# Deformable-convolution stage of a four-layer kernel: block transposes and the second image's offset products change places

## The reference

```python
x = x + L0(gn(x))   # 3-channel offset conv, bilinear sampling, depthwise + pointwise conv
x = x + L1(gn(x))   # 3x3 average pool, then the deformable convolution below
x = x + L2(gn(x))   # 3x3 convolution with masked sign weights
x = x + L3(gn(x))   # striped spatial attention with two 1-d strip kernels
```

```python
xp     = avg_pool3(gn(x))
offset = conv2d(xp, off_w, off_b)            # 18 channels: dy, dx of 9 taps
mask   = 2 * sigmoid(conv2d(xp, mod_w, mod_b))   # 9 channels
# for each tap k and pixel: xp sampled bilinearly at (y + ky - 1 + dy, x + kx - 1 + dx),
# times mask, and out = sum over taps and channels with w; plus bias
```

## Time and profile before

| | |
|---|---|
| median of 3 runs | 1859.02 us (1857.61 to 1861.42) |
| the profiled execution | 1859.19 us |
| its span, first to last instruction | 1857.4 us |
| mean granted TensorE clock | 0.970 |
| busy: TensorE | 1678.3 us (90%) |
| busy: VectorE | 1192.2 us (64%) |
| busy: ScalarE | 603.5 us (32%) |
| busy: GpSimd | 82.9 us (4%) |

### The profile page before, as it was taken

The page is one execution under the profiler, slowest core; times in us unless marked ns, Lnnn a source line. Parts: engine busy times, 40 slices in busy tenths (PEclk is TensorE's granted clock), DMA queues, the critical chain, the costliest instruction groups (busy, mean ns, idle before and its releaser), DMA issues.

```text
span 1857.4 us, 23906 instructions
## 1 busy us (share of the span) xinstructions
PE 1678.3 (90%) x7908; PEld 866.5 (47%) x7908; DVE 1192.2 (64%) x2227; ACT 603.5 (32%) x986; POOL 82.9 (4%) x92
## 2 busy tenths in 40 slices
PE   4968999899998999999998899989999999998876
PEld 2535543455435553364534545355543555435422
DVE  5276359844698358983498734985459835797356
ACT  2134123341324313252242512444133441324222
POOL 1010000100000000000001000010000000000000
PEclk8989999999999999999999999999999999999987
DMA  2000000100000000100001000010000100000000
GB/s 106 12 12 2 1 1 1 48 1 1 1 13 36 1 1 1 43 6 1 1 1 48 2 1 1 1 48 1 1 1 1 47 2 1 1 23 1 1 0 23
DMA packets 7121, 22.97 MB, mean 12 GB/s; under 512 B 1233, under 2 KB 1937, under 8 KB 6929
## 3 DMA queue, kind: packets, MB, share of 16 engines
q1 hardware_dynamic: 6928, 20.58, 3.0%
HBM read 12.19 MB, written 8.39 MB: 11 GB/s over the span
## 4 chain that ended last, share of the span: by engine, by line
issue 74%; PE 16%; DVE 4%; POOL 3%; ACT 2%; POOLq 0%; DVEq 0%; ACTq 0%
PE psN L460 3%; PE psO L460 2%; POOL gst L418 2%; PE psO L486 2%; PE psN L806 1%; PE psN L486 1%; PE psN L561 1%; PE ps L470 1%; PE psN L682 1%; PE psO L682 1%; POOL strip L426 1%; ACT xq L890 1%; PE psN L590 1%; DVE samp L1518 1%; ACT samp L890 1%
## 5 line engine op out<-in xcount | busy, mean ns | idle before, releaser
L486 PE MATMUL psO<-samp,w 128*128 128x512 f32 x576 | 273.5, 605 | 20.8 <-ACT samp L890 20.8
L486 PE MATMUL psN<-xn,w 128*128 128x512 f32 x576 | 277.4, 605 | 5.9 <-issue 4.5
L590 PE MATMUL psN<-GQt,xq 64*128 64x144 f32 x2048 | 169.8, 305 | 25.2 <-ACT samp L890 24.2
L890 ACT ACTIVATE samp<-psN 128x576 f32<-128x576 f32 x256 | 154.2, 649 | 89.2 <-PE psN L590 87.8
L590 PEld LDWEIGHTS psN<-GQt,xq 64*128 64x128 f32 x2048 | 141.1, 190 | 56.8 <-ACT samp L890 42.1
L486 PEld LDWEIGHTS psO<-samp,w 128*128 128x128 f32 x576 | 100.5, 190 | 116.0 <-issue 104.2
L1053 ACT ACTIVATE samp<-psN,vec 128x512 f32<-128x512 f32 x160 | 110.1, 688 | 130.1 <-PE psN L806 130.1
L1217 DVE COPY xblk<-psN 120x256 f32<-120x256 f32 x128 | 54.3, 424 | 149.1 <-PE psN L526 148.8
L486 PEld LDWEIGHTS psN<-xn,w 128*128 128x128 f32 x576 | 98.8, 189 | 87.3 <-issue 85.1
L682 PE MATMUL psN<-img,w 128*128 128x512 f32 x288 | 134.1, 611 | 4.5 <-PE psO L544 4.5
L682 PE MATMUL psO<-img,w 128*128 128x512 f32 x288 | 132.9, 603 | 0.0
(11 more groups left out here) (142 smaller groups left out, 2328.6 us busy)
## 6 DMA issues: line engine op xcount, KB each, us to landing
xin<-in_x SPq DMA_DIRECT2D x16, 512.0 KB, 4.0
out<-yout SPq DMA_DIRECT2D x16, 512.0 KB, 3.5
w<-in_w SPq DMA_DIRECT2D x2, 576.0 KB, 5.4
samp<-in_r SPq DMA_DIRECT2D x1, 576.0 KB, 7.1
tab<-in_tab SPq DMA_DIRECT2D x1, 494.0 KB, 4.9
kh_w<-in_kh SPq DMA_DIRECT2D x1, 320.0 KB, 5.4
kv_w<-in_kv SPq DMA_DIRECT2D x1, 320.0 KB, 5.7
woT<-in_woT SPq DMA_DIRECT2D x1, 256.0 KB, 6.5
```

Source lines behind the costliest of these rows:

```text
L486: last = mm(dst[:, h, :], wgt[:, k, :], rhs(h, k), start=(k == 0), stop=(k == K9 - 1))
L590: last = mm(pair(u)[:, g, :].rearrange("p (k r c) -> p k r c", k=K9, c=SW)[:, :, :, cols], xQ[rows, t, a, e, :], w[rows, e, :, :, cols], s ...
L890: return nc.scalar.activation(out, in_, ACT.Copy)
```

## The change

TensorE waits for both outputs of the previous pass directly behind `offset_parts(2)`, and does blocks 0 and 1 before `offsets(2)`, blocks 2 and 3 behind it, and blocks 4 to 7 behind `doubles(0)`. Only then come `offset_parts(3)` and `far(2)`. `offsets(3)` moves from ahead of the branch into `near(0)`, behind the second step of tile 3; ahead of the branch TensorE now waits for its input (`parts_ready`). ScalarE copies blocks 0 to 3 behind `parts(2)`, then makes the mask, then copies blocks 4 to 7, then does `parts(3)`; for image 1 its order is as before. VectorE does `store_ready(1)` directly behind `store_ready(0)`, ahead of the box sums of image 1. The signal `y_ready` begins at 1 in place of 2, since its value "one of the two" is no longer waited for.

```diff
--- before.py
+++ after.py
@@ -229,7 +229,7 @@
         weights_ready = sem("weights_ready")
         w2_landed = sem("w2_landed")
         x_landed = [Signal(sem(f"x_landed{s}"), 16, 0) for s in range(2)]
-        y_ready = signal("y_ready", 2, 2)
+        y_ready = signal("y_ready", 2)
         yout_free = signal("yout_free", 2)
         y_stored = [Signal(sem(f"y_stored{s}"), 16, 0) for s in range(2)]
 
@@ -700,23 +700,26 @@
                 pe.wait_ge(added.sem, added.at(i, 2))
                 pe.wait_ge(pooled_ready.sem, pooled_ready.at(i, 1))
                 offset_parts(2, img[0], w1off)
+
+                pe.wait_ge(y_ready.sem, y_ready.at(i, 0))
+                blocks(i, 0, (0, 1))
                 offsets(i, 2, 27)
+                blocks(i, 0, (2, 3))
                 doubles(i, 0)
-
-
-                pe.wait_ge(y_ready.sem, y_ready.at(i, -1))
+                blocks(i, 0, range(4, TILES))
+
                 pe.wait_ge(pooled_ready.sem, pooled_ready.at(i, 2))
                 offset_parts(3, img[1], w1off)
                 far(i, 2)
 
-                pe.wait_ge(y_ready.sem, y_ready.at(i, 0))
-                blocks(i, 0, range(TILES))
-                offsets(i, 3, 27)
+                pe.wait_ge(parts_ready.sem, parts_ready.at(i, 4))
                 for s in range(2):
 
                     wait_apart(pe, (added, added.at(i, 2)), (far_ready, far_ready.at(i, s + 2)))
                     is_far = pe.value_load(flag[s][0:1, 0:1])
                     with pe.If(is_far > 0):
+                        if s == 0:
+                            offsets(i, 3, 27)
 
                         pe.wait_ge(g_strips.sem, g_strips.at(i, s + 1))
                         image_T(s, g_xTp)
@@ -730,7 +733,7 @@
 
                         pe.sem_inc(q_smp.sem, STEPS)
                     with pe.Else():
-                        near(i, s)
+                        near(i, s, lambda t: offsets(i, 3, 27) if s == 0 and t == 3 else None)
 
                         pe.wait_ge(q_smp_sb.sem, q_smp_sb.at(i, STEPS * (s + 1)))
 
@@ -981,17 +984,17 @@
                 order = EVENTS if more else LAST
                 parts(i, 2)
                 for s in range(2):
-                    if s:
-                        blocks(i, s, range(2))
+                    early = 2 if s else 4
+                    blocks(i, s, range(early))
                     act.wait_ge(om2_ready.sem, om2_ready.at(i, s + 1))
                     for e in range(PAIRS):
                         ins = nc.scalar.activation(mk[s][:].rearrange("p (t e k) -> p t e k", e=PAIRS, k=K9)[:, :, e, :],
                                                    om2[:, e, 2, :].rearrange("p (t k) -> p t k", k=K9),
                                                    ACT.Sigmoid)
                     ins.then_inc(mask_ready.sem, 1)
+                    blocks(i, s, range(early, TILES))
                     if s == 0:
                         parts(i, 3)
-                    blocks(i, s, range(2 * s, TILES))
                     if s and more:
                         normalise(i, "S0", order)
                         wide(i + 1, 0, i, order)
@@ -1604,10 +1607,10 @@
                     affine_scale(own, "L1B", order)
                     pool3(own, 0, 3, i, order)
                 store_ready(0)
+                store_ready(1)
                 if more:
                     for part in range(4):
                         pool3(own, 1, part, i, order)
-                store_ready(1)
                 if more:
                     assert own.n == DVE_STEPS, own.n
```

## The result

The changed kernel takes 1879.98 us, the median of 4 runs (1877.19 to 1881.84), beside 1858.38 us for the kernel before on the same chip (4 runs, 1857.61 to 1861.42). The ratio is 1.0112, with a 95% interval of 1.0093 to 1.0131: slower by 21.6 us. The forecast was 1884 us in a range of 1864 to 1900. The profiled execution took 1877.19 us, with a span of 1875.3 us and a mean granted clock of 0.965.

What follows compares the result with a forecast made beforehand. TensorE's list was taken to bound the kernel, VectorE's chain having 2.45 us to spare. Eight passes of 1.35 us (10.8) and 1.74 us (13.9) gave +24.7 us on 1859.2 us: 1884 us, range 1864 to 1900.

Steps and rivals of the forecast that it cites:

- TensorE's list isn't the path any more: Ahead of near(0): blocks and parts leave TensorE's path; VectorE's chain, as long, becomes the path; TensorE idles 570.3 to 575.1.
- make `doubles` late: Blocks 2 and 3 behind offsets(2): doubles starts 0.4 us late, VectorE's chain 0.2 us late, with 0.4 as bound.
- The strip copy blocks the hats for 1.95 us: GpSimd's second strip copy, let go earlier, falls inside VectorE's hats and delays them by 1.95 us.
- `near(0)` starts 0.2 us earlier: Start of the sampling: VectorE has tile 0 ready at 575.05, so near(0) starts at 575.1 instead of 575.33.
- `offsets(3)` inside costs 1.55 us: In near(0): these products cost 1.80 us and save a wait of about 0.25, so +1.55 us.
- +1.35 a pass: Convolution over samples: starts at 589.8 instead of 588.48, put at 1.35 us later in each pass.
- The clock loss of 1.74 us a pass: In near(0): after 4.8 us of TensorE idling the clock falls once each pass, +1.74 us; bounds 0 and 3.5.
- A: Rival: no clock loss in the sampling, only the first term, 1870 us; chance 0.17.
- B: Rival: a second clock loss from offsets(3) in the middle of near(0), +13.9 us on top, 1898 us; chance 0.20.
- C: Rival: strip copy doesn't delay the hats; 1854 us without clock loss (chance 0.09), 1868 us with one (0.08).
- D: Rival: no effect, the losses and the gains of C cancel, 1859 us; chance 0.05.

Runs made afterwards that it cites:

- experiment 1: The changed kernel, with GpSimd's strip copy for image 1 waiting until all eight GQt tiles of image 0 are made: 1866.43 us, ratio 1.0034.
- experiment 11: The kernel before the change, with the strip copy of image 1 waiting until the eight GQt tiles of image 0 are made: 1859.50 us, ratio 1.0000.
- the filled kernels: The changed kernel with five or four extra thrown-away products behind far(2), in TensorE's idle stretch: 1877.16 us with five, 1870.72 us with four.
- experiment 2: The changed kernel, with offsets(3) put back ahead of the branch, in front of near(0): 1869.43 us, ratio 1.0052.
- experiment 3: The changed kernel with both the late strip copy for image 1 and offsets(3) back ahead of near(0): 1850.98 us, ratio 0.9954.

## Why the prediction was right

*TensorE's list isn't the path any more: right.* Blocks 0 and 1 cost nothing, `offset_parts(3)` took 4.64 us at the full clock, and the second store and its wait cost nothing. Blocks 2 and 3 didn't make `doubles` late (9.69 us into the pass against 9.88), since VectorE's bias add came later than they did; why is told at the end.

*The strip copy blocks the hats for 1.95 us: right*, 1.86 in the profile, and experiment 1 takes it out and gets 1.56 us a pass. This was the main step, and experiment 11 shows the other half, that the same copy had been nearly free. The Trainium skill, "SBUF — State Buffer", section "Who interferes with whom", has VectorE and GpSimd share a pair of ports under an exclusive lock, and has a VectorE instruction with at most one SBUF input, outside the 2-port modes, stay clear of it. The trace agrees: whichever of the two came first held the other up, in both orders (3.82 us for VectorE's step, 3.90 for the copy), and the two stores with one operand in PSUM took 1.24 us each beside the copy.

*`near(0)` starts 0.2 us earlier: right to 0.2 us in the third pass* (24.19 against 24.18), and equal in the mean, 23.59 against 23.57.

*`offsets(3)` inside costs 1.55 us: right*, 1.62 by the filled kernels (14.77 - 13.15) and 1.68 by experiment 2. (The forecast's +1.35 a pass is 1.32 by its own terms, 589.8 - 588.48, which is 0.2 us in the total.)

*The clock loss of 1.74 us a pass: the mechanism right, the size off.* It is 1.58 in the mean. The 1.74 was read from the sixth pass before the change (14.89 - 13.15), and only about 1.2 us of it are the clock's. In that pass `near(0)` starts 1.6 us earlier, and its second tile 2.07 us behind the first instead of 1.51. The clock was still at 1.00; the tile waited for its `GQt`, which the strip copy had held up (TensorE, then VectorE):

```profile
1240.83 11.54 PE L590 MATMUL psN<-GQt,xq 64*128 64x144 f32 x112 [0.82 <-ACT samp L890]
```

```profile
1239.93 0.77 DVE L1460 STREAM_TRANSPOSE GQt<-GTs 128x576 f32<-128x576 f32 x1
```

The profile names ScalarE's copy, but the first sample copy, for which this step waits, was done by 1240.3 (it began at 1239.57 and takes 0.65), and `GQt` at 1240.70. So the copy wasn't free in the last three passes, and that 1.74 came out near 1.58 is partly luck: after the change the low clock lasts longer in most passes than the 3.4 us it lasted there.

I also summed the loss on the third pass, where the sampling of the kernel before loses nothing. But it took 1.74 us more in its sixth and seventh pass and 0.83 more in its last, together 0.54 us in the mean over eight. In the last the clock is at 1.00; there the second tile waits for its `GQt` too, and the tiles behind it come every 1.59 us instead of 1.51, for a reason that no run shows:

```profile
1684.42 1.25 PE L590 MATMUL psN<-GQt,xq 64*128 64x144 f32 x16 [0.73 <-DVE GQt L1460]
```

```profile
1682.40:1696.40 14.00, 10.04 (x129) 8.48 (x129) 10.55 (x15) 9.54 (x16) 0.67 (x1) 1.00 0.01 2
```

The net is 1.58 - 0.54 = 1.04. This is the term that was mis-sized: (0.02 + 1.62 + 1.04) x 8 = 21.4 us, where 21.6 were measured and 24.7 forecast. It was 0.70 us a pass too high, and part of that was luckily made up by `near(0)`, which was forecast 0.23 us earlier and starts 0.02 later.

*Rivals.* A (no clock loss) is what the filled kernels show, not what happened. B (a second loss through `offsets(3)`): experiment 2, without it inside, saves hardly more than its own length, and in no pass of the changed kernel does the clock fall between `offsets(3)` and the convolution, so no. C failed at its point: the hats lost 1.86 us, and it needed under 0.6. D (no effect) is outside the interval of the measured ratio. The forecast named the two costs, the held hats and `offsets(3)` inside the sampling; experiments 1 and 2 together take out both, and the kernel is then faster than before.

## What to carry to other kernels

When work is moved off the engine that sets the time, look at what its early end lets go on the other engines: here a copy that had been waiting for it fell upon the chain that was next in line, with 2.45 us to spare. Before filling a place inside a latency-bound loop, see whether the same work fits in front of it, where the engine will now be idle. And price an idle stretch of TensorE at its length plus what the clock costs behind it, here 1.58 us a pass behind 4.8 us of idling.

## What the runs showed of the hardware that was not expected

VectorE takes up to 1.87 us from the last instruction of one turn of the loop to the first of the next, with its input at hand: in the third pass the bias add stands 1.87 us behind the last box sum, though `offsets(2)` was done 1.45 us earlier (the row of 562.75 above). In the last pass, which is written out behind the loop, the same add comes 0.49 us behind:

```profile
1682.31 1.23 DVE L1281 TENSOR_TENSOR img<-img,pool_v 128x1024 f32<-128x1024 f32 x1
1684.03 0.38 DVE L1393 TENSOR_TENSOR om<-ps,offb 128x216 f32<-128x216 f32 x1 [0.49 <-PE ps L470]
```

In the three passes in which `offset_parts(2)` runs at the full clock inside the loop (the third, fourth and seventh; 1.77 to 1.87 us), this and not TensorE sets the start of the chain. That it is the turn of the loop is read from its absence in the last pass; no run takes it apart. The clock losses also aren't fixed to a place. In the kernel before they change between `offset_parts(3)` and the sampling from pass to pass, and in the kernel of experiment 3 they stay in the sampling in five passes of eight and come again later in three.
